# Last group of a gated delta rule kernel: output products set between the mixing products and gating moved to VectorE, with small reorderings at the groups' borders and in the first group

## The reference, cut to what matters

```python
qkv = x @ w_qkv
z = (x @ w_z).reshape(Bb, Ss, NVH, HV)
h = jnp.swapaxes(qkv, 1, 2)
conv = jax.lax.conv_general_dilated(h, conv_w[:, None, :], (1,), [(KS - 1, 0)], feature_group_count=CONV_DIM)
conv = jax.nn.silu(conv)
...
core = chunk_gated_delta_rule(q, k, v, g, beta)
out = core * jax.lax.rsqrt(jnp.mean(core * core, -1, keepdims=True) + EPS) * norm_w
out = out * jax.nn.silu(z.astype(jnp.float32))
out = out.astype(x.dtype).reshape(Bb, Ss, VAL_DIM)
return out @ w_out
```

## Time and profile before

| | |
|---|---|
| median of 3 runs | 1457.67 us (1454.42 to 1459.4) |
| the profiled execution's own time | 1459.27 us |
| its span | 1457.5 us |
| PE busy | 1371.9 us (94%) |
| DVE busy | 1079.8 us (74%) |
| ACT busy | 853.3 us (59%) |
| POOL busy | 461.6 us (32%) |
| mean granted clock of PE | 0.988 |

### The profile page before, as it was taken

How to read it: one execution, slowest core, us unless ns; L and a number is a source line. 1 busy time by engine, 2 the same in 40 slices (tenths; PEclk the granted TensorE clock), 3 DMA queues, 4 the chain that set the end, 5 groups by cost and what they waited for, 6 DMA issues and landing times.

```text
span 1457.5 us, 22073 instructions
## 1 busy us (share of the span) xinstructions
PE 1371.9 (94%) x7888; PEld 770.4 (53%) x7888; DVE 1079.8 (74%) x2468; ACT 853.3 (59%) x1745; POOL 461.6 (32%) x375
## 2 busy tenths in 40 slices
PE   0969999999999999999999999988999999999998
PEld 0534754754664574575475476484444444445443
DVE  8888899889889889989988988954598765612000
ACT  4577677678577668767767857755534333212432
POOL 5151161161152134126107016215154344100432
PEclk9999999999999999999999999989999999998999
DMA  3120040030021022003004002102374344100220
GB/s 107 46 90 16 16 123 15 2 123 15 17 76 62 17 66 73 16 20 118 16 2 133 4 17 76 33 17 93 88 213 123 96 127 116 58 0 0 75 99 29
DMA packets 39092, 88.70 MB, mean 61 GB/s; under 512 B 5384, under 2 KB 25352, under 8 KB 37840
## 3 DMA queue, kind: packets, MB, share of 16 engines
q1 hardware_dynamic: 38704, 87.23, 19.7%
q10 hardware_dynamic: 288, 0.14, 0.1%
HBM read 84.77 MB, written 2.59 MB: 60 GB/s over the span
## 4 chain that ended last, share of the span: by engine, by line
PE 75%; DVE 15%; ACT 4%; issue 3%; DMA 1%; POOL 1%; DVEq 0%; ACTq 0%; SPq 0%; POOLq 0%
PE bank L512 13%; PE bank L1807 12%; PE bank L1785 11%; PE bank L574 5%; PE bank L1906 5%; PE bank L549 4%; PE bank L611 4%; PE bank L626 4%; DVE m L1174 3%; DVE conv L1077 3%; PE bank L541 3%; PE bank L606 2%; DVE m L1178 2%; PE bank L617 2%; PE bank L628 2%
## 5 line engine op out<-in xcount | busy, mean ns | idle before, releaser
L1077 DVE SCALAR_TENSOR_TENSOR conv<-bank,taps,conv 128x510 f32<-128x510 f32 x366 | 270.6, 743 | 27.6 <-ACT conv L817 18.3
L512 PE MATMUL bank<-rT,wf 128*128 128x512 f32 x512 | 254.7, 612 | 6.2 <-DVE conv L1088 4.3
L1657 POOL TENSOR_TENSOR ffn_weighted<-ffn_relu,ffn_wide 128x512 f32<-128x512 f32 x96 | 128.3, 1368 | 305.5 <-PE bank L1807 152.9
L1807 PE MATMUL bank<-ffn_weighted,feat 128*128 128x512 f32 x400 | 187.1, 596 | 3.8 <-POOL ffn_weighted L1657 3.8
L1785 PE MATMUL bank<-rT,feat 128*128 128x512 f32 x400 | 190.6, 604 | 0.0
L1668 ACT ACTIVATE ffn_relu<-bank 128x512 f32<-128x512 f32 x100 | 59.6, 596 | 188.1 <-PE bank L1785 188.1
L1320 POOL TENSOR_TENSOR sq<-sq,qsq 128x512 f32<-128x512 f32 x64 | 82.9, 1296 | 270.5 <-ACT sq L1003 269.9
L512 PEld LDWEIGHTS bank<-rT,wf 128*128 128x128 f32 x512 | 89.9, 191 | 87.7 <-issue 74.2
L1807 PEld LDWEIGHTS bank<-ffn_weighted,feat 128*128 128x128 f32 x400 | 76.1, 191 | 100.4 <-issue 98.7
L1785 PEld LDWEIGHTS bank<-rT,feat 128*128 128x128 f32 x400 | 77.0, 194 | 95.3 <-issue 94.8
L574 PE MATMUL bank<-rT,wz 128*128 128x512 f32 x256 | 115.2, 603 | 8.6 <-DVE m L1178 7.6
(11 more groups left out here) (235 smaller groups left out, 2614.8 us busy)
## 6 DMA issues: line engine op xcount, KB each, us to landing
z<-decay_rows SPq DMA_DIRECT2D x64, 384.0 KB, 3.9
ffn_wide<-ffn_shares SPq DMA_DIRECT2D x64, 256.0 KB, 5.3
feat<-in_L_chunks_dram SPq DMA_DIRECT2D x25, 512.0 KB, 4.2
wf<-in_wf_dram SPq DMA_DIRECT2D x8, 1024.0 KB, 4.8
wz<-in_wz_dram SPq DMA_DIRECT2D x8, 512.0 KB, 3.7
wo<-in_wo_dram SPq DMA_DIRECT2D x8, 512.0 KB, 3.7
ffn_wide<-ffn_shares SPq DMA_DIRECT2D x8, 512.0 KB, 4.0
m<-in_fT_dram SPq DMA_DIRECT2D x2, 512.0 KB, 5.1
```

The lines of the kernel that those rows point to most:

```text
L512: ins = pe.matmul(banks[bank_of(p, n)][:], wf[:, c, ORDER[n // NH], :], rT[:, c, halves(n % NH)], start=(c == 0), stop=(c == CT - 1))
L1077: dve.scalar_tensor_tensor(acc[:, :, k:], src[:, :, 0:T - k], taps[:, ORDER[n // NH], KS - 1 - k:KS - k], acc[:, :, k:], ALU.mult, ALU.add ...
L1657: pool.tensor_tensor(hw[:, j, u, :], h2[:, j, u, :], wide[:, j, u // NH % BLOCKS, halves(u % NH)], ALU.mult).then_inc(weighted, 1)
L1807: last = pe.matmul(banks[4 + 2 * c + h][:], chunk[:, slot, CT + t, c * P:(c + 1) * P], of, start=start, stop=stop, skip_group_check=True)
```

## The change

There are four parts.

In the last group PE runs a new function, `last_mixes`. Its mixes use three banks (`mix_bank`: banks 0 to 2) and all its sums one (`rms_bank`: bank 3), so that banks 4 to 7 are free for the four output parts, two products of which (both channel tiles of one unit) follow the sum of iterations 4 to 7. The 16 products behind the groups are gone. In the last group DVE gates each unit behind its normalize (`gated_last`), and POOL only adds.

At the seven borders PE issues output products 0 and 1 ahead of gram 1, and each of the later ones one iteration earlier.

In the first group POOL masks the first two decay rows ahead of clearing `pT`, and ACT spreads its first four block copies over n = 5, 6 and 7.

Ahead of the first group ACT applies its taps of units 4 and 5 earlier.

```diff
+    def mix_bank(g, n):
+        return banks[n % 3 if g == NG - 1 else 2 + n % 4]
+
+    def rms_bank(g, n):
+        return banks[3 if g == NG - 1 else 6 + n % 2]
...
+        def last_mixes(g):
+
+            def outputs(n):
+                for c in range(CT):
+                    u = c * NH + n % NH
+                    output(g, u, 4 + u, n // NH)
+
+            for n in range(NU):
+                if n < 4:
+                    pe.wait_ge(evicted, g * EVICTS + 16 + n + 1)
+                if n >= 3:
+                    pe.wait_ge(og_ready, g * NU + n - 2)
+                mix(g, n)
+                if n >= 2:
+                    if n >= 3:
+                        pe.wait_ge(ln_done, g * NU + n - 2)
+                    rms(g, n - 2)
+                if n == 4:
+                    pe.wait_ge(out_added, g * 4)
+                if n >= 4:
+                    outputs(n - 4)
+            for n in (NU - 2, NU - 1):
+                pe.wait_ge(ln_done, g * NU + n)
+                rms(g, n)
+                outputs(n - 2)
+            for n in (NU - 2, NU - 1):
+                outputs(n)
...
                 pe.wait_ge(og_ready, before - 1)
-                output(g - 1, 0, 4, 0)
+                for v in range(2):
+                    output(g - 1, 0, 4, v)
                 pe.wait_ge(conv_ready, (g + 1) * NF * NH)
...
                 if not first:
-                    if n == GV:
+                    k = n + 1
+                    if k == GV:
                         pe.wait_ge(og_ready, before)
-                    output(g - 1, n // GV, 4 + n // GV, n % GV)
+                    if k < 2 * GV:
+                        output(g - 1, k // GV, 4 + k // GV, k % GV)
...
         groups(pe, group)
-        for u in (0, 2, 1, 3):
-            if u < 2:
-                pe.wait_ge(og_ready, NG * NU - 1 + u)
-            else:
-                pe.wait_ge(ln_done, NG * NU - 3 + u)
-            for v in range(GV):
-                output(NG - 1, u, 4 + u, v)
...
-                if n == 5:
+                if not first and n == 5:
                     take_blocks(g, 0, range(0, 4), 8)
+                elif first and n >= 5:
+                    take_blocks(g, 0, range(0, 4), 8, ((0,), (1,), (2, 3))[n - 5])
...
         own_tap(0, 3)
+        own_tap(0, 4)
         silu(0, 0)
         silu(0, 1)
+        own_tap(0, 5)
         square_k(0, 0)
-        own_tap(0, 4)
         silu(0, 2)
-        own_tap(0, 5)
...
+        def gated_last(g, n):
+
+            out = zs[:, n // NH, halves(n % NH)]
+            dve.wait_ge(og_ready, g * NU + n + 1)
+            dve.tensor_tensor(out, out, rs[:, n % 3, :], ALU.mult).then_inc(gated, 1)
...
                     normalize(g, n - 1)
+                    if last_group:
+                        gated_last(g, n - 1)
...
             if first:
+                pool.wait_ge(front["heads_in"], 80)
+                for n in range(AHEAD):
+                    hide(0, n)
                 pool.wait_ge(heads_done, 1)
                 pool.wait_ge(front["rows_out"], 32)
                 pool.memset(pT[:], 0.0).then_inc(zeroed, 1)
-                pool.wait_ge(front["heads_in"], 80)
-                for n in range(AHEAD):
-                    hide(0, n)
...
-                if n >= 2:
+                if n >= 2 and g < NG - 1:
                     multiply(g, n - 2)
```

More of the change, by code:

```diff
@@ L540, in rms @@
             pe.wait_ge(sum_ready, g * NU + n + 1)
-            pe.matmul(banks[6 + n % 2][:], ones[:], sq[:, n % 3, :], start=True, stop=True).then_inc(rms_full, 1)
+            pe.matmul(rms_bank(g, n)[:], ones[:], sq[:, n % 3, :], start=True, stop=True).then_inc(rms_full, 1)
         def output(g, u, b, v):
@@ L622, in mix @@
             v, h = n // NH, n % NH
-            b = banks[2 + n % 4]
+            b = mix_bank(g, n)
             for i in range(2):
@@ L750, in group @@
                 solve(v, 1)
+            if last_group:
+                last_mixes(g)
+                return
             for n in range(NU):
@@ L761, in group @@
                         pe.wait_ge(ln_done, g * NU + n - 3)
-                    elif not last_group:
+                    else:
                         pe.wait_ge(lk_done, p * GK + n - 1)
-                    else:
-                        pe.wait_ge(out_added, g * 4 + n - 3)
                     rms(g, n - 2)
-                if not last_group and n >= 1:
+                if n >= 1:
                     project_v(p, n - 1)
@@ L773, in group @@
             rms(g, NU - 2)
-            if not last_group:
-                project_v(p, NU - 1)
+            project_v(p, NU - 1)
             pe.wait_ge(ln_done, g * NU + NU - 2)
@@ L863, in decays, with take_blocks @@
                 act.activation(e[:, T:], e[:, T:], ACT.Exp, bias=gcol[:, v, 2 * s + 1:2 * s + 2]).then_inc(dec_ready, 1)
-        def take_blocks(g, kh, seqs, after):
+        def take_blocks(g, kh, seqs, after, quads=range(4)):
             act.wait_ge(m_ready, g * PAIRS + after)
             t0, t1 = 2 * seqs[0], 2 * seqs[-1] + 2
-            for q in range(4):
+            for q in quads:
                 r = slice(q * SB, (q + 1) * SB)
@@ L882, in root @@
             act.wait_ge(rms_full, g * NU + n + 1)
-            act.activation(rs[:, n % 3, :], banks[6 + n % 2][:], ACT.Ln, scale=1.0 / HD, bias=EPSQ).then_inc(ln_done, 1)
+            act.activation(rs[:, n % 3, :], rms_bank(g, n)[:], ACT.Ln, scale=1.0 / HD, bias=EPSQ).then_inc(ln_done, 1)
             act.wait_ge(ln_done, g * NU + n + 1)
@@ L1002, in group @@
                 act.wait_ge(mix_full, g * NU + n + 1)
-                act.activation(sq[:, n % 3, :], banks[2 + n % 4][:], ACT.Square).then_inc(sq_ready, 1)
+                act.activation(sq[:, n % 3, :], mix_bank(g, n)[:], ACT.Square).then_inc(sq_ready, 1)
                 if n >= 2:
@@ L1113, in normalize @@
             r = rs[:, n % 3, :]
-            dve.scalar_tensor_tensor(r, banks[2 + n % 4][:], norm_w[:, 0:1], r, ALU.mult, ALU.mult).then_inc(og_ready, 1)
+            dve.scalar_tensor_tensor(r, mix_bank(g, n)[:], norm_w[:, 0:1], r, ALU.mult, ALU.mult).then_inc(og_ready, 1)
+        def gated_last(g, n):
+            out = zs[:, n // NH, halves(n % NH)]
+            dve.wait_ge(og_ready, g * NU + n + 1)
+            dve.tensor_tensor(out, out, rs[:, n % 3, :], ALU.mult).then_inc(gated, 1)
         def slice_part(k, u):
@@ L1304, in vector @@
         normalize(NG - 1, 7)
+        gated_last(NG - 1, 7)
     def last_sum(dve, k):
@@ L1379, in group @@
                     hide(g + 1, n + AHEAD - NU)
-            for n in (NU - 2, NU - 1):
-                multiply(g, n)
+            if g < NG - 1:
+                for n in (NU - 2, NU - 1):
+                    multiply(g, n)
         for g in range(NG):
```

1 line of the change is left out of this document (removed).

## The result

Over 20 runs each the changed kernel takes 1461.14 us (1457.94 to 1467.44) and the kernel before 1456.24 us (1453.45 to 1462.24): ratio 1.0033, 95% interval 1.002 to 1.0046. That is 4.9 us slower. The profiled execution took 1465.40 us, 6.1 more than that of before.

A forecast was written before the change was run, and what follows sets the result against it. PE, busy 94% of the span, was taken to bound the kernel. Terms 3.0 + 3.3 - 0.5 - 0.5 gave +5.3 us, forecast 1463.0 us; own range 1460.7 to 1466.2, wider range 1456.5 to 1467.

The forecast's parts named there:

- The last group's mixes: Last group: output products end 2.9 us later and the router starts later; +3.0 us at full clock.
- The ring: Last group: normalize k releases mix k + 3, then sum k + 1, then normalize k + 1; 4.73 us per unit.
- gating on DVE costs nothing: Last group: gating takes some 0.7 us behind a normalize, 3.3 us ahead of the next, so adds nothing.
- The clock: Last group: PE's idle time lowers the granted clock to 0.50 over mix 3 and sum 1; +3.3 us, bounds 0 and 4.6.
- one of two cases: Last group: low clock lasts over mix 4 and sum 2 too, another 2.3 us beyond mix 3 and sum 1.
- one length of idle time: Granted clock on PE: idling 2.09 us had lowered it and 1.98 had not, so 3.4 us was expected to.
- The borders: Group borders: the moved product fills PE's wait, but part 2 waits for DVE; 0.1 at five borders, -0.5 us.
- The first group: First group: masks ahead of the clearing let `m` start 0.3 earlier, block copies give 0.2; together -0.5 us.
- That the clock holds: Rival, last group: same chain but PE keeps clock 1.00; 2.0 us slower, 1459.7, no change; chance 0.14.
- That the products hide in the waits: Rival, last group: mixes keep their pace and output products fill PE's idle time; 4.5 us faster, 1453.2; chance 0.10.
- The borders in full: Rival, group borders: DVE takes gram 5 earlier, each border gives 0.47; sum +2.5, 1460.2, no change; chance 0.07.
- wait for both masks: Rival, first group: DVE's copies wait for both masks and the clearing delays what follows; 1.4 us more, 1464.4; chance 0.07.

The follow-up runs named there:

- the filled kernel: Changed kernel plus five unread products on PE, three between sum 0 and mix 3, two between sum 1 and mix 4; 1461.46 and 1458.6 us, ratios 1.0037 and 1.0014.
- the unfilled ring: Last group's new order without unread products: changed kernel twice (1.0033, 1.0037), last group alone (1.0023), and two trace-only variants, gating on POOL and masks behind copies.
- the kernel with the last group alone: Kernel before with only `last_mixes`, its banks and `gated_last` added; 1460.49 us, ratio 1.0023 to the kernel before.
- the kernel with the sums ahead: Changed kernel with sum n-2 ahead of mix n on PE and root n-2 ahead of square n on ACT; 1454.05 us, ratio 0.998 to before.

## Why the prediction was right

I had forecast 1463.0 us, 5.3 above before, slower or nearly so. Measured was 1461.14, 4.9 above. (Of the 1.9 us between them 1.4 lie in the kernel before, which has 1456.24 in 20 runs and had 1457.67 in three.)

**The last group's mixes** (predicted +3.0): shown. With the clock held, the stretch is 33.26 us, 3.40 more than 29.86. The ring was as read: mix 7 starts 19.68 us behind normalize 0 (987.98 to 1007.66 in the filled kernel; 19.73 predicted), and the products end at 1020.40, 32.42 behind it (32.5 predicted). The missing 0.4 is at the border, where I took 0.4 us to the router and it is 0.84. The step that was too short is "gating on DVE costs nothing": DVE gates unit 7 until 1022.8, so it adds the first quarter at 1022.97 although PE had it by 1022.3 (three products behind 1019.7). With gating on POOL the router waits 0.26 instead of 0.84, but PE waits 0.20 for the gating and its products end later, so only 0.1 us is net.

**The clock** (predicted +3.3, bounds 0 and 4.6): shown in the traces. Over the five traces of the unfilled ring the first two turns exceed twice 4.72 by 3.20, 3.40, 1.69, 4.46 and 4.46 us, 3.4 in the mean; filled, twice by nothing. That the clock is low over mix 4 and sum 2 I had as one of two cases; it was in all five, in two without coming back in between, in two after a second fall, and in one it fell only there. I had judged it by one length of idle time, 2.09 us enough and 1.98 not. That rule doesn't hold: 3.36 us left it high in the kernel with the last group alone, and 2.26 us at 1060.34 in the changed one. The timed runs' mean clocks put the clock's part in the whole program at 1.3 to 2.8 us, so the 3.4 is shown for this stretch in traced executions only.

**The borders** (predicted -0.5, bounds 0 and -3.3): the mechanism is right, the size too small. The waits for `conv_ready` went, and 3.0 us of waits for `m` stand in their place. I took 0.1 us at five borders; the traces have 0.2 at each of seven, 1.5 us in all. The timed runs can't tell it.

**The first group** (predicted -0.5): some -0.4 in traces. `m` starts at 76.72 instead of 76.97, and I had 76.65. The rule of the Trainium skill (SBUF — State Buffer, Who interferes with whom), that a VectorE instruction with two SBUF inputs contends only with a GpSimd instruction that reads SBUF, holds in the trace: the product of `bcol` and `u`, both in SBUF, ran at 76.50 in 0.18 us in the midst of the clearing (73.46 to 76.97), while it had taken 0.50 beside a mask. With the rule alone I would have said 76.5. What made `m` later than that is that the first copy waited 1.03 us where I had 0.8. Of the block copies little came, since ACT has as many to do: the transposition that waits for them starts at 107.09, and at 107.43 before, 0.34 us earlier where `m` was 0.25 earlier.

**The sum.** +3.4 + 3.4 - 1.9 = +4.9 by the traces, and +2.8 to +4.3 with the clock's part as the timed runs have it, against a measured +4.9 (2.9 to 6.7 by the interval). The size of the clock's part in an ordinary run is the least certain of the three. That the forecast came within 0.4 us of the measured difference is partly luck: the ring cost 0.4 us more than said, the borders gave 1.0 more, and the clock's 3.3 is the middle of two values.

**The rivals.** That the clock holds would be the filled kernel's trace; unfilled it was seen in no trace. That the products hide in the waits did not happen here and happens once sum and mix change places: I had put it as turning on whether a sum stands ahead of the first mix that waits for a normalize, and the kernel with the sums ahead shows this point to be the right one. The borders in full would be 3.3 us, and the traces have 1.5. The copies didn't wait for both masks; only the first copy waited.

## What to carry to other kernels

Before an engine's queue gets new work between two steps, draw the ring through all engines: which result releases the next instruction, and what stands in the queue between it and the step that closes the ring. Here, as the traces read, one bank fewer turned two interleaved rings into one. Work put into the waits left the turns at 4.72 us; the order of two instructions on each of two engines brought them to 3.88. A wait on TensorE can cost more than its length, so look at the granted clock behind it, and take two or three traces, as one trace can show it high by chance. Where the mean clock of every run is kept, compare that too: here the times of one and the same kernel differ by 8 us along with it.

## What the runs showed of the hardware

Unneeded work made a stretch shorter in two traces of two: with five products, 4.3 us on PE, put into waits, normalize 0 to the router took 33.26 us where it had been 36.47. The whole kernel's time doesn't show it. The same idle time of 3.36 us left the granted clock at 1.00 in one trace and lowered it to 0.50 in four. And a small instruction can be dear by its neighbour: a copy of 128 by 32 that takes 0.18 us took 1.21 us as it started 0.10 us into a product of POOL, and put what stood behind it on DVE back by 1.0 us, while a two-operand product of the same size ran unhindered inside POOL's clearing of 3.51 us.
